# Two source tiles share one 16-bit column of counts in a graph network's aggregation

## The reference

```python
h = relu(layernorm(x)); x = x + L0(h, src, dst, edge_attr)   # per-edge messages, tanh, summed by target
h = relu(layernorm(x)); x = x + L1(h)   # three GCN layers
h = relu(layernorm(x)); x = x + L2(h)   # three rounds of normalised sums over edges
h = relu(layernorm(x)); x = x + L3(h)   # sum over edges, two dense layers

# what L1, L2 and L3 have in common, seven times in all:
agg = segment_sum(h[src], dst, num_segments=12500)
```

## Time and profile before

| | |
|---|---|
| median of 3 runs | 9491.55 us (9488.19 to 9496.71) |
| span of the profiled execution | 8056.5 us |
| own time of that execution | not listed; the median is 1435 us above the span |
| TensorE busy | 7250.3 us, 90% |
| VectorE busy | 3022.3 us, 38% |
| ScalarE busy | 2022.9 us, 25% |
| GpSimd busy | 1563.6 us, 19% |
| bytes moved | 1927.15 MB, mean 239 GB/s |

### The profile page before, as it was taken

One profiled execution on the slowest core, in us unless ns is written; L12 is line 12 of the kernel. 1 busy time (PEld: TensorE's weight loads), 2 busy tenths in 40 slices (PEclk: granted clock), 3 DMA queues, 4 the chain that ended last, 5 costly groups with the idle time before them and its releaser, 6 DMA issues. The chain is left out here.

```text
span 8056.5 us, 132776 instructions
## 1 busy us (share of the span) xinstructions
PE 7250.3 (90%) x44520; PEld 4945.0 (61%) x44520; DVE 3022.3 (38%) x4630; ACT 2022.9 (25%) x3278; POOL 1563.6 (19%) x1655
## 2 busy tenths in 40 slices
PE   4688888888888888888779999999999999999999
PEld 2577777777777777777645555555555555555554
DVE  5566666666666666666540000011100000011000
ACT  3344444444444444444300000000000000000000
POOL 2334433443443344334200000000000000000000
PEclk9799999999999999999889999999999999999999
DMA  3688888888888888888758787877788888888776
GB/s 103 164 213 213 217 210 214 214 217 211 214 216 213 213 214 217 211 214 214 174 200 281 268 281 268 280 269 279 272 295 289 295 289 290 293 290 293 266 267 228
DMA packets 828957, 1927.15 MB, mean 239 GB/s; under 512 B 66366, under 2 KB 123134, under 8 KB 828862
## 3 DMA queue, kind: packets, MB, share of 16 engines
q1 hardware_dynamic: 775564, 1816.94, 74.5%
q0 software_dynamic: 52352, 108.63, 4.3%
q10 hardware_dynamic: 946, 0.26, 0.0%
HBM read 1752.16 MB, written 173.46 MB: 239 GB/s over the span
## 5 line engine op out<-in xcount | busy, mean ns | idle before, releaser
L1199 PE MATMUL ps_a<-ring,table 128*128 128x448 fp8e4 x19208 | 3656.3, 353 | 42.8 <-DVE table L105 42.8
L1199 PEld LDWEIGHTS ps_a<-ring,table 128*128 128x128 f16 x19208 | 1881.8, 98 | 1793.4 <-DVE table L105 44.4
L593 ACT CAST unit<-ps_c 128x490 fp8e4<-128x490 f32 (+1 forms) x2548 | 1641.0, 662 | 1994.7 <-PE ps_c L734 1976.0
L560 POOL DMA_INDIRECT gathered<-u_source,plan x1576 | 1486.8, 943 | 2326.9 <-PE ps_u L756 1773.9
L734 PE MATMUL ps_c<-cell_hot,lane_hot 128*128 128x490 f16 x2548 | 889.2, 370 | 490.5 <-DVE cell_hot L643 490.5
L643 DVE TENSOR_SCALAR cell_hot<-iota_n,cell 128x490 f16<-128x490 f16 x2548 | 728.3, 343 | 378.4 <-PE ps_c L734 378.3
L1023 ACT COPY agg<-ps_a 128x448 f32<-128x448 f32 x196 | 104.3, 532 | 2930.3 <-PE ps_a L1199 2930.3
L773 PEld LDWEIGHTS ps_m<-M_sb,z 128*128 128x128 f32 x6272 | 810.2, 192 | 34.5 <-issue 0.3
L773 PEld LDWEIGHTS ps_m<-M_sb,x_sb 128*128 128x128 f32 x6272 | 810.0, 192 | 13.1
L997 POOL COPY hst<-h 128x896 f32 x28 | 26.4, 943 | 3925.8 <-PE ps_t L1211 2463.0
L773 PE MATMUL ps_m<-M_sb,x_sb 128*128 128x64 f32 x6272 | 784.7, 268 | 0.0
(11 more groups left out here) (185 smaller groups left out, 3302.1 us busy)
## 6 DMA issues: line engine op xcount, KB each, us to landing
ring<-counts SPq DMA_DIRECT2D x392, 1848.0 KB, 7.1
ring<-counts SPq DMA_DIRECT2D x196, 1792.0 KB, 7.0
basis<-in_basisT SPq DMA_DIRECT2D x198, 1024.0 KB
x_sb<-in_basisT SPq DMA_DIRECT2D x198, 1024.0 KB
counts<-unit SPq DMA_DIRECT2D x196, 784.0 KB
dst_all<-in_dst_seq SPq DMA_DIRECT2D x198, 512.0 KB
gathered<-u_source,plan POOLq DMA_INDIRECT x1576
window<-u_target SPq DMA_DIRECT2D x198, 64.0 KB
```

The lines of the kernel that those rows point to most:

```text
L560: pool.indirect_dma_start(gathered[q][:, i, :], None, Us, bass.IndirectOffsetOnAxis(ap=T["plan"][:, at:at + 1], axis=0)).then_inc(S[f"rows ...
L593: nc.scalar.copy(unit[q][:, :, BD * i:BD * i + n], got[:, :, 0:n], saturate=False).then_inc(S["emptied"], 1)
L1199: last = mm(ps_a[:, b, 0:BC].rearrange("p (u c) -> p u c", u=BU), table[n % 2][:, k, :], cells, start=(k == 0), stop=(k == TILES - 1))
```

## The change

Two neighbouring source tiles now share a cell. `cell` becomes 5 x (source tile / 2) + place, so `cell_hot` has 49 x 5 = 245 columns (`CELLS`). An edge from an even tile is worth 1, one from an odd tile 256: a second code, `worth`, is made in the preparation and multiplied in by the same instruction that writes `cell_hot`. The sum in PSUM is then count_even + 256 x count_odd, and ScalarE writes it as a 16-bit integer. Its two bytes are the two counts. The dense stage reads such a byte as an 8-bit float; the code n stands for n / 512 there, for the counts that occur, so the sums are multiplied by 512 (`1 / CODE`) in the copy at L1023. A matmul of L1199 reads every second byte of a row, the low or the high one. The parts of the source tiles are 34, 32 and 32 in place of 33, 33 and 32, so that each is even. The bytes of A stay the same.

The diff, cut to its core:

```diff
-PARTS = [(0, 33), (33, 66), (66, 98)]
+PAIRS = TILES // 2
+PARTS = [(0, 34), (34, 66), (66, 98)]
+CELLS = PAIRS * BD
+ODD = 256.0
+CODE = 2.0 ** -9
...
-            nc.vector.tensor_scalar(part[:, :, :], ends[:, :, :, 0], 7, None, ALU.logical_shift_right)
+            nc.vector.tensor_scalar(part[:, :, :], ends[:, :, :, 0], 8, None, ALU.logical_shift_right)
...
+            ch(nc.vector.tensor_scalar(part[:, :, :], ends[:, :, :, 0], P, None, ALU.bitwise_and))
+            nc.vector.scalar_tensor_tensor(out=far[:, :, :], in0=part[:, :, :], scalar=ODD / P, in1=far[:, :, :], op0=ALU.mult, op1=ALU.add).then_inc(S["cell"], 1)
...
+            dve.wait_ge(S["turned_ev"], BQ // 4)
+            ch(nc.vector.tensor_scalar(T["worth"][:, :], T["cell"][:, :], ODD - 0.5, ODD, ALU.is_gt, ALU.mult))
+            ch(nc.vector.tensor_tensor(T["cell"][:, :], T["cell"][:, :], T["worth"][:, :], ALU.subtract))
+            ch(nc.vector.tensor_scalar(T["worth"][:, :], T["worth"][:, :], 1.0 - 1.0 / ODD, 1.0, ALU.mult, ALU.add))
...
-        cell_hot = [sb(f"cell_hot{i}", [P, TILES * BD], F16) for i in range(RING)]
-        unit = two(sb, "unit", [P, TILES, UC], F8)
+        cell_hot = [sb(f"cell_hot{i}", [P, CELLS], F16) for i in range(RING)]
+        unit = two(sb, "unit", [P, PAIRS, UC], U16)
...
-                        got = ps_c[(UB * q + i) % 2][:, 0:TILES * BD].rearrange("p (k j) -> p k j", j=BD)
-                        nc.scalar.copy(unit[q][:, :, BD * i:BD * i + n], got[:, :, 0:n], saturate=False).then_inc(S["emptied"], 1)
+                        got = ps_c[(UB * q + i) % 2][:, 0:CELLS].rearrange("p (k j) -> p k j", j=BD)
+                        nc.scalar.copy(unit[q][:, :, BD * i:BD * i + n], got[:, :, 0:n]).then_inc(S["emptied"], 1)
...
-                        nc.vector.tensor_scalar(cell_hot[i % RING][:, :], T["iota_n"][:, :], T["cell"][:, bass.ds(g * UB + i, 1)], None, ALU.is_equal).then_inc(S["cells"], 1)
+                        nc.vector.tensor_scalar(cell_hot[i % RING][:, :], T["iota_n"][:, :], T["cell"][:, bass.ds(g * UB + i, 1)], T["worth"][:, bass.ds(g * UB + i, 1)], ALU.is_equal, ALU.mult).then_inc(S["cells"], 1)
...
-                        mm(ps_c[(UB * q + i) % 2][:, 0:TILES * BD], lane_hot[q][:, i, :], cell_hot[i % RING][:, :], start=True, stop=True).then_inc(S["counted"], 1)
+                        mm(ps_c[(UB * q + i) % 2][:, 0:CELLS], lane_hot[q][:, i, :], cell_hot[i % RING][:, :], start=True, stop=True).then_inc(S["counted"], 1)
...
-        ring = sb("ring", [P, SLOTS, BU, PARTS[0][1], UC], U8)
+        ring = sb("ring", [P, SLOTS, BU, PARTS[0][1] // 2, UC], U16)
...
-                    nc.scalar.copy(agg[:, BC * b:BC * b + BC], ps_a[:, b, 0:BC]).then_inc(S["agg_out"], 1)
+                    nc.scalar.mul(agg[:, BC * b:BC * b + BC], ps_a[:, b, 0:BC], 1.0 / CODE).then_inc(S["agg_out"], 1)
...
-                        cells = ring[:, s, :, k - k0, :].bitcast(F8)
+                        cells = ring[:, s, :, (k - k0) // 2, :].bitcast(F8).rearrange("p u (c h) -> p u c h", h=2)[:, :, :, k % 2]
```

More of the change, by code:

```diff
@@ L8 @@
 F8 = mybir.dt.float8e4
+U16 = mybir.dt.uint16
 I32 = mybir.dt.int32
@@ L109, in build @@
     x = w["x"]
-    A = nc.dram_tensor("counts", (A_BYTES,), U8, kind="Internal").ap()
+    A = nc.dram_tensor("counts", (A_BYTES // 2,), U16, kind="Internal").ap()
     Us = nc.dram_tensor("u_source", (NP, 2 * D), F32, kind="Internal").ap()
@@ L117, in build @@
     G = {"messages": messages, "rows": rows16, "irregular": irregular, "src": w["srcT"], "dst": w["dstT"]}
-    A_units = A.rearrange("(u p k c) -> u p k c", u=UNITS, p=P, k=TILES)
+    A_units = A.rearrange("(u p k c) -> u p k c", u=UNITS, p=P, k=PAIRS)
     with ExitStack() as ctx:
@@ L138, in build @@
             T["lane"] = esb("lane", [P, BQ * P + UB], F16)
-            T["iota_n"] = esb("iota_n", [P, TILES * BD], F16)
+            T["iota_n"] = esb("iota_n", [P, CELLS], F16)
+            T["worth"] = esb("worth", [P, BQ * P], F16)
             prepare(nc, T, x, w, Us, Ud, irregular)
@@ L166, in prepare @@
         iota_i = sb("iota_i", [P, W + 1 + BQ], I32)
-        iota_c = sb("iota_c", [P, TILES * BD], I32)
+        iota_c = sb("iota_c", [P, CELLS], I32)
         iota_p = sb("iota_p", [P, 1], F32)
@@ L226, in _ @@
             nc.gpsimd.iota(iota_i[:, W + 1:W + 1 + BQ], pattern=[[P, BQ]], base=0, channel_multiplier=1).then_inc(S["iotas"], 1)
-            nc.gpsimd.iota(iota_c[:, :], pattern=[[1, TILES * BD]], base=0, channel_multiplier=0).then_inc(S["iotas"], 1)
+            nc.gpsimd.iota(iota_c[:, :], pattern=[[1, CELLS]], base=0, channel_multiplier=0).then_inc(S["iotas"], 1)
             nc.gpsimd.memset(x_sb[:, TILES - 1, :], 0.0).then_inc(S["xinit"], 1)
@@ L363, in _ @@
             ch(nc.vector.tensor_tensor(far[:, :, :], far[:, :, :], near[:, :, :], ALU.add))
-            nc.vector.scalar_tensor_tensor(out=far[:, :, :], in0=part[:, :, :], scalar=float(BD), in1=far[:, :, :], op0=ALU.mult, op1=ALU.add).then_inc(S["cell"], 1)
+            ch(nc.vector.scalar_tensor_tensor(out=far[:, :, :], in0=part[:, :, :], scalar=float(BD), in1=far[:, :, :], op0=ALU.mult, op1=ALU.add))
+            ch(nc.vector.tensor_scalar(part[:, :, :], ends[:, :, :, 0], P, None, ALU.bitwise_and))
+            nc.vector.scalar_tensor_tensor(out=far[:, :, :], in0=part[:, :, :], scalar=ODD / P, in1=far[:, :, :], op0=ALU.mult, op1=ALU.add).then_inc(S["cell"], 1)
             dve.wait_ge(S["cell"], 1)
@@ L512, in keep @@
                     sp.sem_inc(S["passed"], 1)
-                    sp.dma_start(A_units[bass.ds(g, 1), :, :, :].rearrange("u p k c -> p (u k c)"), unit[q][:, :, :].rearrange("p k c -> p (k c)").bitcast(U8)).then_inc(S[f"kept{q}"], 16)
+                    sp.dma_start(A_units[bass.ds(g, 1), :, :, :].rearrange("u p k c -> p (u k c)"), unit[q][:, :, :].rearrange("p k c -> p (k c)")).then_inc(S[f"kept{q}"], 16)
                 load(0, 0, 0)
@@ L913, in dense @@
         rows = sb("rows_d", [P, XT, D], F32)
-        ring_bytes = ring[:, :, :, :, :].rearrange("p s u k c -> p (s u k c)")
-        hot = [ring_bytes[:, 2 * GC * i:2 * GC * (i + 1)].bitcast(F16) for i in range(XT)]
+        ring_words = ring[:, :, :, :, :].rearrange("p s u k c -> p (s u k c)")
+        hot = [ring_words[:, GC * i:GC * (i + 1)].bitcast(F16) for i in range(XT)]
         V = {n: sem("g_" + n) for n in "table ends rows known gathered placed hot used".split()}
@@ L951, in _ @@
                             sp.sem_inc(S["passed"], 1)
-                            block = A_units[bass.ds(g * (BANKS * BU) + j % BANKS * BU, BU), :, k0:k1, :].rearrange("u p k c -> p u k c")
-                            sp.dma_start(ring[:, j % SLOTS, :, 0:k1 - k0, :], block).then_inc(a_in[j % SLOTS], 16)
+                            block = A_units[bass.ds(g * (BANKS * BU) + j % BANKS * BU, BU), :, k0 // 2:k1 // 2, :].rearrange("u p k c -> p u k c")
+                            sp.dma_start(ring[:, j % SLOTS, :, 0:(k1 - k0) // 2, :], block).then_inc(a_in[j % SLOTS], 16)
             with sp.Else():
@@ L1086, in place_edges @@
                     for i in range(XT):
-                        nc.vector.tensor_scalar(hot[i], places[:, :], place[:, i:i + 1], None, ALU.is_equal).then_inc(V["hot"], 1)
+                        nc.vector.tensor_scalar(hot[i], places[:, :], place[:, i:i + 1], CODE, ALU.is_equal, ALU.mult).then_inc(V["hot"], 1)
             def loop(start, body):
```

## The result

The changed kernel takes 9332.34 us (median of 4 runs, 9321.91 to 9336.76); the kernel before takes 9493.82 beside it. The ratio is 0.9827 (0.9813 to 0.9841): 161 us faster, where 252 were forecast.

The account below looks back on a forecast made before the run. Edge stage bound by a chain between VectorE and TensorE, dense stage by TensorE's rate. Columns -200, VectorE -20, clock -34, preparation +2 sum to -252 us: 9491.55 becomes 9240 us, range 9175 to 9350 (forecast's own 9185 to 9295).

Parts of the forecast that it names:

- Rival 1: Edge stage: TensorE's clock falls in every group, +69 us in place of the gain, 9343 us in all; chance 0.14.
- rival 3: Edge stage: transfers take over, loads come late and the period stops near 18.0 us, 9340 us in all; chance 0.05.
- signs of being wrong: Wrong if L1199 grows, cell_hot passes 400 ns, or the edge stage's mean clock is under 0.93.
- TensorE's columns: Edge stage: count matmuls of 245 columns for 490 save 0.102 us in ten blocks a group, 200 us in all.
- VectorE: Edge stage: three half-wide cell_hot a group save 0.033 us each, 20 us in all; bounds -77 and +100.
- The clock: Edge stage: clock falls, 0.70 us each, come in a quarter of groups instead of every second: 34 us gained.
- another period would break the pattern: Edge stage: falls keep step with the groups; with another period they come only when the two happen to meet.
- Preparation: Before the edge stage: added instructions over 2,560 elements, mostly beside other work, cost +2 us; bounds 0 and 10.
- Dense reads: Dense stage: L1199 reading every second byte costs nothing; at the other end each matmul doubles, +3650 us.
- Rival 4: Dense stage: stepped byte reads slow the 19,208 L1199 matmuls; 12,890 us at full doubling, 10,150 at a quarter; chance 0.08.
- Evictions: Edge stage: ScalarE's evictions, 0.66 us each, halve too, but stay under the step and their gain is hidden.
- The 1435 us around the span: Timed median 9491.55 us less the profiled span of 8056.5; claimed to have no part in the change.

Follow-up runs that it names:

- e0: The kernel before, no edit, run for a second trace: 9365.1 us (span 9363.4).
- e5: The changed kernel with one gather per group in place of eight, the other seven tiles zeros: 8034.72 us, ratio 0.9983 to the kernel before.
- e6: The changed kernel with half of the basis rows loaded, the others zeros, all eight gathers kept: 8020.67 us, ratio 0.9971 to the kernel before.
- e1: The changed kernel with cell_hot written 490 wide again, of which the count matmul reads 245: 9192.13 us, ratio 0.982 to the kernel before.
- e2: The changed kernel with cell_hot 490 wide and the count matmul streaming all 490 columns, evictions still 245: 9355.99 us, ratio 0.9996 to the kernel before.
- e11: The changed kernel with one gather per group and twelve more matmuls ahead of block 11: 7814.66 us, ratio 0.9703 to the kernel before.
- e7: The changed kernel without the additions to semaphore passed at each count block on TensorE and ScalarE: 7903.29 us, ratio 0.9817 to the kernel before.
- e8: The changed kernel, unchanged, run again for a trace and times: 9169.98 us, ratio 0.9793 to the kernel before.
- e3: The changed kernel with cell_hot written without the second scalar and its multiplication: 9169.89 us, ratio 0.9799 to the kernel before.
- e10: The kernel before with twelve more matmuls of 245 columns per group ahead of block 11: 9358.04 us, ratio 1.0008 to the kernel before.

## Why the prediction was right, and where it was off

The main term was right: fewer columns in TensorE's part of the group. That the time falls into the stated range is in part luck. The waits were read from a trace in which signals are on time and a group takes 18.8 us; in the executions that were timed it takes over 25. The result lies where rivals 1 and 3 had been placed, and neither describes it. One of the prediction's own signs of being wrong came true: the edge stage's clock is 0.77 and not at least 0.93. Since it is 0.80 in e0, without the change, most of that is the other kind of execution; but in e5 and e6, where signals are on time, it is 0.86 for 0.95.

- **TensorE's columns** (200 us; bounds 0.78 and 1.02 us a group). The step is right, 0.10 us behind the count and a step shorter by 0.10. Of the time it gave 165 us between e1 and e2, 0.84 us a group. Together with VectorE, in groups without a fall, it gave 0.87 us in e11 and 1.01 in e7, so the forecast fits the kind of execution that it was read from. Why only 0.84 came in the other kind is not shown. Some of the ten blocks may lie where a late signal holds the group, and the clock is lower with fewer columns (0.79 in e1, 0.81 in e2).
- **VectorE** (20 us). Nothing came of it: 340 for 343 ns. The width gave 0.06 us, half of the upper bound of 0.13; the second scalar took 0.06, just above the 0.05 read from `from_node`. That price stood in the bound for a loss, but the 0.033 that was taken for the gain was a middle between nothing and a quarter of the pitch, with no term for the scalar.
- **The clock** (34 us gained). This was the wrong step: a fall in "a quarter of the groups". Where signals are on time and the kernel is as in e5, a fall comes in every group and half of the falls last twice as long, and that takes 0.87 us of gain back in full. Where signals are late the clock went from 0.80 (e0) to 0.77 to 0.78 (changed kernel, e8); what that cost was not measured by itself. Rival 1 had the mechanism and the sign, for the reason given there (less work around the same idle time); its price, 0.35 us more per group than now, was too small. The argument that another period would break the pattern was wrong: another pattern with the same sum for two groups took its place.
- **Preparation** (+2). From the last layer-norm instruction to `fault_row` it took 223.69 to 247.13 before and 230.22 to 255.76 now: 2.1 us more. Right.
- **Dense reads** (0). 3655.3 us for 3656.3. Rival 4 is refuted: a step of two bytes costs nothing, as the Trainium skill's passage on cachelines has it (SBUF — State Buffer, "Door 1: The DMA port swizzle").
- **Transfers** (rival 3). No: e6 took half of the basis bytes away and the two groups stayed at 37.5 us.
- **Evictions** (hidden). Nothing speaks against it: e2, with evictions of 423 ns, is no faster than the kernel before, though its `cell_hot` is slower too.
- **The 1435 us around the span** "has no part in the change". Wrong as a reading. An execution has under 2 us around its span (9365.1 against 9363.4 in e0). The gap was the sign that the trace and the timed executions were of different kinds, and the prediction passed over it.

So 252 forecast and 161 measured. Taken apart by the experiments, about 35 us of the columns, 20 of VectorE and 34 of the clock did not come, which leaves 163. The 35 are measured (e1, e2); that the clock's term was nothing where signals are late, and not a loss inside the 35, is only argued.

Open: what makes the signals late. In the traces that have it (e0 to e3, changed kernel, e8 to e10) every late eviction starts within the first 12 us after POOL begins a group's gathers, when the transfer queues are full too; in e7, with the same gathers and bytes, none is late. The experiments meant to part the two ran where no signal is late. Open too: the changed kernel as it stands was not run where signals are on time. e6 (0.9971) and e7 (0.9817) are the nearest to it; which of them it would be like is not shown.

## What to carry to other kernels

When the timed runs and the span of the profiled one differ by more than a few microseconds, take a second trace before costing anything: the steps may be right and the waits around them others. Work taken from TensorE while another engine makes it idle once a round can come back as a lower clock, down to the same period to the last digit, and a small edit can then change the time by more than the work it removes; compare the granted clock of the stage before the busy times, and try a few idle-time matmuls. An operand per partition that is added to a short VectorE instruction costs here as much as 245 of its 16-bit elements.

## What the runs showed of the hardware

- A second per-partition scalar, with its multiplication, costs 58 to 61 ns on VectorE (e1, e3); 245 f16 elements cost 61 to 64 ns, with an odd width too. Two operations with constants leave 0.16 us beside the elements (L380), so it is the scalar that costs.
- TensorE reads every second byte of SBUF as an 8-bit float at full rate: 0.190 us for 448 columns.
- Two unlike kernels settled at the same 37.54 us for two groups through the falls of the clock, with fewer columns at 0.86 for 0.95; twelve matmuls more per group made the second one 220 us faster (8034.72 us in e5, 7814.66 in e11).
- In some comparisons TensorE's additions to semaphores came late, by up to 7.85 us at the count matmuls, and a group took 25.4 us for 18.8 in the same kernel. The same chip number stands for both kinds.
